# Two-layer cross attention on one core: normalising behind the heads, and keys and values from split operands

## The reference

```python
# layer 0: attention over the 256 columns, 64 channels
x_q = einsum('oc,bcn->bno', w_qk, y);  x_k = einsum('oc,bcn->bon', w_qk, x)
x_v = einsum('oc,bcn->bon', w_v, x) + b_v
attention = softmax(einsum('bnc,bcm->bnm', x_q, x_k), axis=-1)
attention = attention / (1e-07 + attention.sum(axis=1, keepdims=True))
x_r = relu(w_t @ (x - x_v @ attention) + b_t);  x = x + x_r
# layer 1: 16 heads of 16, tokens attend to the context's tokens
q = layer_norm(x, ln1) @ q_w + q_b;  k = ctx @ k_w + k_b;  v = ctx @ v_w + v_b
attn = softmax(where(mask, q k^T / 4, min), axis=-1)
hidden = (attn @ v) @ cproj_w + cproj_b + x
y = gelu(layer_norm(hidden, ln2) @ fc_w + fc_b, tanh) @ proj_w + proj_b
return hidden + y
```

## Time and profile before

| | us |
|---|---|
| median of 3 runs | 170.68 (170.66 to 171.85) |
| the profiled execution | 171.03 |
| its span | 169.2 |
| busy PE / PE weight loads | 146.0 / 111.3 |
| busy DVE / ACT / POOL | 101.1 / 98.6 / 87.0 |

### The profile page before, as it was taken

The page is one execution under the profiler, slowest core; times in us unless marked ns, Lnnn a source line. Parts: engine busy times, 40 slices in busy tenths (PEclk is TensorE's granted clock), DMA queues, the critical chain, the costliest instruction groups (busy, mean ns, idle before and its releaser), DMA issues.

```text
span 169.2 us, 3520 instructions
## 1 busy us (share of the span) xinstructions
PE 146.0 (86%) x1260; PEld 111.3 (66%) x1260; DVE 101.1 (60%) x243; ACT 98.6 (58%) x242; POOL 87.0 (51%) x146
## 2 busy tenths in 40 slices
PE   7599999999986888197998665957999999999993
PEld 6365678788754264074675544645787999888993
DVE  2435525897975343990589797795678521488221
ACT  2017977789769755735778667966967333344000
POOL 8935617468888952572431976799361634000000
PEclk9969999999999999759999999999999999999999
DMA  1995320202101200000000000000000010000001
GB/s 50 344 326 175 66 62 0 66 0 62 43 25 62 62 0 0 0 6 0 0 4 6 0 4 0 4 0 0 4 0 0 4 61 32 31 0 6 31 31 62
DMA packets 6786, 6.89 MB, mean 41 GB/s; under 512 B 1044, under 2 KB 6194, under 8 KB 6770
## 3 DMA queue, kind: packets, MB, share of 16 engines
q1 hardware_dynamic: 5808, 5.85, 11.1%
q10 hardware_dynamic: 674, 0.56, 1.0%
q0 software_dynamic: 288, 0.27, 0.9%
HBM read 5.62 MB, written 1.05 MB: 39 GB/s over the span
## 4 chain that ended last, share of the span: by engine, by line
PE 57%; POOL 17%; DVE 9%; issue 7%; DMA 4%; ACT 3%; ACTq 1%; POOLq 0%
PE psum L784 53%; DMA ys<-in_ctx_dram 4%; POOL probs L381 4%; POOL us L344 3%; POOL rstd L308 2%; PE psum L1019 2%; POOL wfc_lo L320 2%; POOL wpj_lo L320 1%; DVE smax L738 1%; POOL hidT_lo L372 1%; POOL rows L325 1%; POOL rows L389 1%; DVE psums L625 1%; DVE probs L749 1%; DVE xn L641 1%
## 5 line engine op out<-in xcount | busy, mean ns | idle before, releaser
L381 POOL TENSOR_TENSOR probs<-probs,pinv 128x512 f32<-128x512 f32 x16 | 16.5, 1055 | 9.7 <-DVE pinv L630 9.7
L344 POOL TENSOR_SCALAR us<-uext,rinv 128x128 f32<-128x128 f32 x32 | 12.4, 399 | 13.9 <-DVE rinv L604 13.3
L784 PE MATMUL psum<-wpj_hi,ff_hi 128*128 128x256 f32 x64 | 18.3, 287 | 0.0
L784 PE MATMUL psum<-wpj_hi,ff_lo 128*128 128x256 f32 x64 | 18.1, 283 | 0.0
L784 PE MATMUL psum<-wpj_lo,ff_hi 128*128 128x256 f32 x64 | 18.1, 283 | 0.0
L398 ACT ACTIVATE ys<-psum,vec 128x512 f32<-128x512 f32 x16 | 10.9, 687 | 9.3 <-PE psum L784 9.2
L683 DVE TENSOR_REDUCE nmax<-psum 128x2 f32<-128x512 f32 x16 | 10.3, 685 | 9.9 <-PE psum L784 9.9
L784 PE MATMUL psum<-att,us 128*128 128x256 f32 x64 | 15.2, 381 | 0.7 <-POOL us L344 0.7
L625 DVE TENSOR_REDUCE psums<-probs 128x8 f32<-128x512 f32 x16 | 10.6, 660 | 8.5 <-ACT probs L540 8.3
L443 ACT ACTIVATE att<-psum,nmax 128x256 f32<-128x256 f32 x32 | 14.7, 471 | 0.3 <-DVE nmax L683 0.2
L784 PE MATMUL psum<-hidT_hi,wfc_hi 128*128 128x512 f32 x32 | 13.2, 414 | 1.1 <-POOL hidT_lo L372 1.1
(11 more groups left out here) (115 smaller groups left out, 367.6 us busy)
## 6 DMA issues: line engine op xcount, KB each, us to landing
wstage<-in_L_xattn_fc_w_dram SPq DMA_DIRECT2D x4, 256.0 KB, 5.2
wstage<-in_L_xattn_proj_w_dram SPq DMA_DIRECT2D x4, 256.0 KB, 2.7
out_dram<-rows SPq DMA_DIRECT2D x8, 128.0 KB, 1.7
ys<-in_ctx_dram SPq DMA_DIRECT2D x1, 512.0 KB, 6.3
rows<-in_x_dram SPq DMA_DIRECT2D x1, 512.0 KB, 7.4
ys<-in_ctx_dram ACTq DMA_DIRECT2D x1, 384.0 KB, 7.0
rows<-in_x_dram SPq DMA_DIRECT2D x1, 384.0 KB, 5.8
wk<-in_L_xattn_k_w_dram SPq DMA_DIRECT2D x1, 256.0 KB, 6.7
```

What stands on the lines that cost most here:

```text
L344: pool.tensor_scalar(us[:, n % 2, e, j, :], uext[:, n % 2, j, e * C:e * C + P], rinv[:, n % 2, e, j:j + 1], 1.0, ALU.mult, ALU.mult).then_ ...
L381: pool.tensor_tensor(half, half, pinv[:, n % 2, k].unsqueeze(2).broadcast_to([P, H // 2, C]), ALU.mult).then_inc(S["probs_ready"], 1)
L784: return pe.matmul(dst, lhsT, rhs, start=start, stop=stop)
```

## The change

The probabilities stay unnormalised. Four more products by `block_ones` give, in the other half of the heads' bank, each head's sum in the place where its outputs lie; ACT takes Ln of the sums and Exp of its negative, and DVE multiplies on the way to `hdT`. The bias of the values goes through `wc` once, as two products by `vb_cols`, and is added to `cproj_b`. `hn` moves from ACT to POOL. Context, key weights and value weights are split into high and low part, in memory that the MLP's activations use later, and each product of keys and values becomes three in f32r.

```diff
@@ buffers
-        wk = sb("wk", [P, G, D])
-        wv = sb("wv", [P, G, D])
-        ctxT = sb("ctxT", [P, G, TOK])
+        block_ones = sb("block_ones", [P, 2, HD])
+        sums_ln, sums_inv = csln, csinv
+        vb_cols = hn[:, 0, :].rearrange("p (g t) -> p g t", g=G)
+        ctxT = [ff[0][:, 0:G, :], ff[1][:, 0:G, :]]
+        wkr = [ff[k][:, 2:3, :].rearrange("p o (g n) -> p (o g) n", g=G) for k in range(2)]
+        wvr = [ff[k][:, 3:4, :].rearrange("p o (g n) -> p (o g) n", g=G) for k in range(2)]
+        CTX_LOW = (4, 6)
@@ gpsimd
-                pool.tensor_scalar(shift[:, n % 2, :], mv[:, n % 2, 0:1], rstd[:, n % 2, :], -1.0, ALU.mult,
-                                   ALU.mult).then_inc(S["hid_shift"], 1)
+                wait(pool, "hid_turned", n - 1)
+                pool.tensor_scalar(hn[:, n % 2, :], rows[:, n, :], mv[:, n % 2, 0:1], rstd[:, n % 2, :], ALU.subtract,
+                                   ALU.mult).then_inc(S["hid_normed"], 1)
+            def weight_low(w, s):
+                wait(pool, f"w{s}_hi", 1)
+                hi, lo = wkr if s == "k" else wvr
+                pool.tensor_tensor(lo, w[:], hi.bitcast(F32), ALU.subtract).then_inc(S[f"w{s}_lo"], 1)
             for t in STEPS:
+                if t == 0:
+                    weight_low(wk, "k")
...
                 if t == 0:
+                    weight_low(wv, "v")
...
-                    for i, k in enumerate(HEAD_HALVES):
-                        wait(pool, "probs_inv", 2 * n + i + 1)
...
@@ scalar
                     wait(act, "heads_made", n + 1)
-                    for g in range(G):
-                        identity(hdT[:, g, :], psum[:, HEADS, g * P:(g + 1) * P], col(V_B + g), 1.0, "heads_ready")
+                    if n == 0:
+                        wait(act, "mix_normed", 2 * N)
+                    wait(act, "heads_ready", n)
+                    act.activation(sums_ln[:], halfbank(HEADS, 1), ACT.Ln).then_inc(S["sums_ln"], 1)
+                    wait(act, "sums_ln", n + 1)
+                    act.activation(sums_inv[:], sums_ln[:], ACT.Exp, scale=-1.0).then_inc(S["sums_inv"], 1)
...
-                    act.activation(hn[:, n % 2, :], rows[:, n, :], ACT.Identity, bias=shift[:, n % 2, :],
-                                   scale=rstd[:, n % 2, :]).then_inc(S["hid_normed"], 1)
@@ vector
+            for b in range(2):
+                for d in range(2):
+                    dve.memset(block_ones[b * C:(b + 1) * C, d, :], float(b == d)).then_inc(block_ready, 1)
+            def heads_normed(n):
+                wait(dve, "sums_inv", n + 1)
+                wait(dve, "attn_made", n)
+                dve.tensor_tensor(hdT[:].rearrange("p g t -> p (g t)"), halfbank(HEADS, 0), sums_inv[:],
+                                  ALU.mult).then_inc(S["heads_ready"], 1)
+            def ctx_low(h, i):
+                wait(dve, "ctx_ready", 2 * h + i + 1)
+                cols = slice(2 * i * P, 2 * (i + 1) * P)
+                dve.tensor_tensor(ctxT[1][:, :, cols]..., bank(FILL)..., ctxT[0][:, :, cols]...,
+                                  ALU.subtract).then_inc(S["ctx_lo"], 1)
+            def weight_high(w, s):
+                dve.wait_ge(w_loaded[s], 16)
+                dve.tensor_copy((wkr if s == "k" else wvr)[0], w[:]).then_inc(S[f"w{s}_hi"], 1)
+                if t == 0:
+                    ctx_low(0, 0)
+                    weight_high(wk, "k")
+                if t == 0:
+                    ctx_low(0, 1)
+                    weight_high(wv, "v")
+                if t in CTX_LOW:
+                    ctx_low(1, CTX_LOW.index(t))
+                if n == 0:
+                    dve.wait_ge(vb_made, 1)
+                    dve.wait_ge(w_loaded["cb"], 16)
+                    dve.tensor_tensor(cproj_b[:], halfbank(WTX, 1), cproj_b[:], ALU.add).then_inc(attn_b_ready, 1)
-                if 0 <= n < N:
-                    sum_of_probs(n, 0)
+                if 0 <= t - AT - 1 < N:
+                    heads_normed(t - AT - 1)
                 if 0 <= t - AT - 2 < N:
                     hidden_mean_var(t - AT - 2)
-                if 0 <= n < N:
-                    inverse_of_sum(n, 0)
-                    sum_of_probs(n, 1)
-                    inverse_of_sum(n, 1)
@@ tensor
                 if kind == "keys":
-                    pe.wait_ge(w_loaded["k"], 16)
-                    wait(pe, "ctx_ready", 2 * (h + 1))
+                    wait(pe, "wk_lo", 1)
+                    wait(pe, "ctx_lo", 2 * (h + 1))
                     for c in range(G):
-                        ins = mm(bank(FILL), wk[:, c, k * P:(k + 1) * P], ctxT[:, c, :], c == 0, c == G - 1)
+                        for a, b in ((0, 0), (0, 1), (1, 0)):
+                            ins = mm(bank(FILL), wkr[a][:, c, k * P:(k + 1) * P], ctxT[b][:, c, :],
+                                     c == 0 and a + b == 0, c == G - 1 and a == 1)
...
                     for a in range(2):
                         tok = slice((2 * k + a) * P, (2 * k + a + 1) * P)
                         for c in range(G):
-                            ins = mm(halfbank(FILL, a), ctxT[:, c, tok], wv[:, c, :], c == 0, c == G - 1)
+                            for x, y in ((0, 0), (0, 1), (1, 0)):
+                                ins = mm(halfbank(FILL, a), ctxT[x][:, c, tok], wvr[y][:, c, :],
+                                         c == 0 and x + y == 0, c == G - 1 and x == 1)
...
+                if n == 0:
+                    pe.wait_ge(w_loaded["c"], 16)
+                    pe.wait_ge(vb_cols_ready, G)
+                    for c in range(G):
+                        ins = mm(halfbank(WTX, 1), vb_cols[:, c, :], wc[:, c, :], c == 0, c == G - 1)
+                    ins.then_inc(vb_made, 1)
...
+                    for j in range(J):
+                        ins = mm(psum[32 * j:32 * (j + 1), HEADS, D:2 * D], block_ones[:].rearrange("p b d -> p (b d)"),
+                                 prT[:, j * G:(j + 1) * G, :].rearrange("p g t -> p (g t)"))
                     ins.then_inc(S["heads_made"], 1)
...
-                        wait(pe, "probs_ready", 2 * n + i // (HP // 2) + 1)
+                        wait(pe, "probs_exp", 2 * n + i // (HP // 2) + 1)
```

More of the change, by code:

```diff
@@ L114, in xattn_two_layers @@
         rstd = sb("rstd", [P, 2, 1])
-        shift = sb("shift", [P, 2, 1])
         xn = sb("xn", [P, 2, D])
@@ L329, in x1_plus_bias @@
                 if n == 0:
-                    pool.wait_ge(w_loaded["cb"], 16)
+                    pool.wait_ge(attn_b_ready, 1)
                     pool.wait_ge(w_loaded["pb"], 16)
@@ L416, in fill @@
                     wait(act, "values_made", 2 * h)
-                    act.copy(ctxT[:, :, 2 * i * P:2 * (i + 1) * P].rearrange("p g (a t) -> p a g t", a=2),
+                    act.copy(ctxT[0][:, :, 2 * i * P:2 * (i + 1) * P].rearrange("p g (a t) -> p a g t", a=2),
                              bank(FILL).rearrange("p (a g t) -> p a g t", a=2, g=G)).then_inc(S["ctx_ready"], 1)
@@ L549, in _ @@
                     queries_bias(1, 1)
-                n = t - AT - 2
-                if 0 <= n < N:
-                    wait(act, "hid_shift", n + 1)
-                    wait(act, "hid_turned", n - 1)
-                    act.activation(hn[:, n % 2, :], rows[:, n, :], ACT.Identity, bias=shift[:, n % 2, :],
-                                   scale=rstd[:, n % 2, :]).then_inc(S["hid_normed"], 1)
                 mlp_units(t + 0.6)
@@ L618, in relu_in @@
                 wait(dve, "relu_out", n - 1)
+                if n == 0:
+                    dve.wait_ge(vb_made, 1)
+                    dve.wait_ge(w_loaded["cb"], 16)
+                    dve.tensor_tensor(cproj_b[:], halfbank(WTX, 1), cproj_b[:], ALU.add).then_inc(attn_b_ready, 1)
                 dve.tensor_tensor(rin[:, n % 2, :], halfbank(WTX, 0), mixn[:],
                                   ALU.subtract).then_inc(S["relu_in"], 1)
-            def sum_of_probs(n, i):
-                wait(dve, "probs_exp", 2 * n + i + 1)
-                half = probs[:, n % 2, i * BANK:(i + 1) * BANK].rearrange("p (h k) -> p h k", k=C)
-                dve.tensor_reduce(psums[:, n % 2, HEAD_HALVES[i]], half, AX.X, ALU.add).then_inc(S["probs_sum"], 1)
-            def inverse_of_sum(n, i):
-                wait(dve, "probs_sum", 2 * n + i + 1)
-                wait(dve, "probs_ready", 2 * (n - 1))
-                dve.reciprocal(pinv[:, n % 2, HEAD_HALVES[i]],
-                               psums[:, n % 2, HEAD_HALVES[i]]).then_inc(S["probs_inv"], 1)
+            def heads_normed(n):
[6 more added lines that the diff above has]
+                cols = slice(2 * i * P, 2 * (i + 1) * P)
+                dve.tensor_tensor(ctxT[1][:, :, cols].rearrange("p g (a t) -> p a g t", a=2),
+                                  bank(FILL).rearrange("p (a g t) -> p a g t", a=2, g=G),
+                                  ctxT[0][:, :, cols].bitcast(F32).rearrange("p g (a t) -> p a g t", a=2),
```

(15 more changed lines are left out.)

24 lines of the change are left out of this document (10 added, 14 removed).

## The result

The changed kernel takes 174.85 us (median of 4 runs, 174.59 to 175.08) against 170.67 of the kernel before: a ratio of 1.0224, 95% interval 1.0172 to 1.0275. The forecast was 175.9, in a range of 171.0 to 179.0. The profiled execution took 175.08 us with a span of 173.1, 3.9 more than before's 169.2.

The account below looks back on a forecast made before the run. It took DVE's own round to bound the attention's rounds, with PE nearly never idle in the MLP. Front 2.8, middle -0.6 and tail 3.0 sum to 5.2 us on a 169.2 span: 174.4, hence 175.9 us, range 171.0 to 179.0.

Parts of the forecast that it names:

- the 179.8 of the split products: Rival, keys and values: split products don't run in one pass, +1.3 us a unit, 179.8 us; chance 0.03.
- rival of six costlier loads, 183.6: Rival, tail: a table change costs a second 1.28 us per load; with six loads 183.6; chance 0.06 with four-load case.
- The front: Start to first queries: 1.3 us to E(3), tile 3's energies, plus DVE stalls of 0.85 and 0.65; 2.8 us later.
- the stall of step 4: DVE waits for ACT's copy before subtracting, ahead of the next maxima; 0.85 us comes through.
- that of step 6: The same DVE wait for ACT's copy at step 6; of 2.0 us, 0.65 comes through.
- The middle: First queries to the MLP's first product: the attention's rounds and POOL's removed multiplications give 0.6 us.
- 5.53 us a round: Attention's rounds: ACT's ring of heads, Ln, Exp, hidf, hi, exps and prT sets 5.53 us, against 5.72 before.
- The tail: MLP's first product to first projection's result: six more ACT table loads, 7.7 us on ACT, cost 3.0 us.
- the rival with a costlier change of table: Tail: each load costs a second 1.28 us; 179.0 us with four loads, 183.6 with six; chance 0.06.
- Faster: Rival, rounds: they shrink to 4.4 us by what DVE loses, the middle gives 7.2; 167.8 us; chance 0.10.
- Small price: Rival, front and tail: Ln and Exp share a load, POOL's queue covers both DVE stalls; 172.4 us; chance 0.20.
- The sums lie side by side: Heads: the sums' four products add 0.43 us; rival, they don't, 1.3 more per H in five rounds, 182.4; chance 0.07.

Follow-up runs that it names:

- p2: The kernel before with only the split products of keys and values, attention as before: 173.71 us, ratio 1.0121.
- e1: The changed kernel with the two context subtractions of half 1 one step later in DVE's queue, behind the maxima, gx and uext: 173.47 us, ratio 1.0131.
- x2: The changed kernel without the two vb products and their addition, leaving the values' bias out: 174.22 us, one execution.
- q1: The kernel before with only x1_plus_bias of all tiles moved to step 8 on POOL: 171.51 us, ratio 1.0040.
- x1: The changed kernel with the four products of the sums issued twice, writing the same values: 178.9 us, one execution.
- e2: The changed kernel with the joint Ln and Exp table loaded ahead of Ln for the last two tiles: 174.21 us, ratio 1.0153.

## Why the prediction was right

Its sum was 5.2 and the span grew by 3.9. The direction and the mechanism of the three big terms held; the middle was mis-sized by 1.1 us and the tail by 0.3, and the term behind the tail, put at nothing, is 0.4. (A slip besides: the range to 179.0 leaves out the 179.8 of the split products too, and its own rival of six costlier loads, 183.6.)

**The front, 2.8: measured 2.74.** By steps: E(3) 1.09 late for 1.3, the stall of step 4 1.07 for 0.85, that of step 6 0.58 for 0.65. `p2` and `e1` show that the stalls are the order of DVE's queue. The 1.3 has nearly the right pieces: the late start of keys unit 0 (E(1) +1.14), what the split products give back, and the vb products (0.86 in `x2`). The gain of a keys unit was priced at 0.35 (1.63 for 1.98), and the trace has just that; but keys unit 1's was called hidden and came through: E(1) to E(2) is 0.61 shorter, twice the 0.3 of the values unit.

That the 1.09 lies so near is partly luck. From the start to E(1) a profile repeats badly: 15.59 us in the kernel before and 16.62 in `q1`, whose edit comes later; 16.06 to 17.31 in the changed kernel and the runs with its first steps. E(1) to E(3) repeats to 0.02 us: 13.49 in both of the former, 13.42 to 13.44 in the latter. So behind E(1) the vb products and what the split products give back cancel, and the price is that of the late start: E(0) to E(1) is 5.20 to 5.71 us in the four profiles without split products and 6.09 to 6.93 in the nine with them, 1.0 more in the mean.

**The middle, -0.6: measured -1.70.** This term was mis-sized most, and in it the "5.53 us a round". The mechanism was right: ACT's ring took DVE's place, with H released by `prT`, and `x1` shows that it is the bound. The size was off by 0.34. `hidf` to the end of `prT` was put at 3.25 and is 3.23; H to Ln at 1.18 and is 1.15; but Ln and Exp were put at 0.8 and are 0.75 together, and `prT` to H at 0.3 "(the waits of H are five in a row)" and is 0.06: `prT` is the first of the five, and the four behind it, met by then, take no time that shows. Over three rounds that is 1.0 us, and 1.2 with the 5.6 that the forecast's H(5) holds: the whole miss of 1.1. The first two rounds, put at 6.4 and 5.1, are 6.34 and 5.01. The dip of the clock is 7 us long in both profiles, so it takes no part in this difference; with a short one Q to H(0) is 0.8 us less (`e1`, `x2`) and with a long one 1.7 more (`x1`). `hn` on POOL took 1.23 us and not the 0.73 assumed, with no effect on the rounds, as POOL idles half of each.

**The tail, +3.0: measured +3.29.** Six loads of 1.28 us, each with one function's instructions behind it. From the MLP's start to the last gelu's end it was put at 20.15 and is 20.21; from there to the projection's result at 1.7 and is 1.95. The Trainium skill (ScalarE: Activation LUTs, "What ACT_TABLE_LOAD costs") adds a drain of about 1380 ns to each load. The trace has 0.03 us or less on either side of all seven loads, so the rival with a costlier change of table falls. The Trainium skill (ScalarE: Activation LUTs, "Table sets: the hidden batching unit") says that Ln and Exp need one load as one set holds both. That is so only where that set is named: left to the placement, the pair took two loads, and in `e2`, with the set loaded by hand, one. With four loads the forecast put the tail 2.0 lower; `e2` measured 1.43, as ACT then waits for PE.

**Behind the tail, 0: measured -0.38.** The forecast said that PE's work there is unchanged, and it is; its instructions follow each other more closely (last section), and the cause stays open.

**The rivals.** "Faster", by DVE's relief, was priced on a round of 4.4; the rounds are 5.19, as ACT's ring says. "Small price" needed both stalls covered and one load per pair; neither is so, but it is what `e1` and `e2` make of the kernel. The sums lie side by side, and the split products run in one pass (0.235 us apart), so those two fall as well.

## What to carry to other kernels

When a bound engine is relieved, add up the ring that closes next, instruction by instruction from the rows of before, and charge nothing for a wait that is already met (four of them took 0.06 us here). Look at what a moved function does to ACT's tables where it lands among another function's calls: here a pair of 0.4 us instructions carried three loads of 1.28 us each. On an engine that idled before they cost less than their sum (7.7 us of loads, 3.3 us of tail), and taking them away gives back less too (2.06). A consumer put into an in-order queue directly behind its producer's time costs the whole wait (1.65 us here), and nothing one step later; and what a stall, a load or a first round costs can be won back one by one, which made of a change that lost 2.2% one that wins 1%. Before a difference of a few tenths between two profiles is called a price, look for the same stretch in every profile at hand, and at the granted clock in it.

## What was not expected of the hardware

- GpSimd's `tensor_scalar` over 128x256 f32 with two per-partition operands took 1.23 us (`hn`), where its `tensor_tensor` over the same shape took 0.73 or 0.74 on average in each of its four groups.
- DVE's reciprocal of 128x256 from PSUM took 1.75 us, four times the 0.42 of a multiplication of that size.
- The granted clock falls to 0.50 between 69 and 85 us, in a stretch in which PE waits 3.7 us for DVE's softmax, and doubles the products behind it (3.78 for 1.98 us). Its length, 3, 7 or 10 us, differs between profiles with the same code there. Dips of 3 us stand elsewhere in some profiles: between 7 and 12 us in five of them, the kernel before among these, in `q1`'s third round and in `p2`'s fifth. They are part of what scatters the executions of one kernel and not all of it: of 19 executions of the kernel before, the 8 with a mean granted clock near 0.98 took 170.8 us in the mean and the 11 near 0.968 took 171.8, and either group spreads over 2.8 us. So stretches of a trace compare better than whole times, once the clock in them is known to be the same.
- The second half's projections follow each other at 2.80 us in every kernel with the attention's part (and 31.26 from the first result to the last), and at 2.88 in the kernel before, in `p2` and in `q1`; instruction starts lie 0.117 and 0.120 apart. The instructions, their shapes and the granted clock (1.00) are the same. It is worth 0.4 us, and its cause stays open: no run was made for it.
